# Rotary embedding by chunks with rows along the PSUM bank, its sine product moved to GpSimd, in a four-layer one-core Trainium2 kernel

## What is computed

```python
# layer 3; layer 1 adds a bias to q, k, v; layer 2 pairs even and odd elements of a head
q = x @ Wq   # 32 heads of 16;  k = x @ Wk, v = x @ Wv: 8 heads of 16
def rope(x):                      # before the scores, on q and k, not on v
    x1, x2 = x[..., :8], x[..., 8:]
    return concat([x1 * cos - x2 * sin, x2 * cos + x1 * sin])
out = softmax(causal(rope(q) @ rope(k).T / 4)) @ v @ Wo
```

## Time and profile before

| what | value |
|---|---|
| three runs, median | 2409.13 us (2407.0 to 2411.66) |
| profiled execution, its own time | 2416.49 us |
| its span | 2414.8 us |
| mean granted clock of PE | 0.963 |
| busy: PE, DVE, ACT, POOL | 2254.6, 1464.6, 1183.2, 506.3 us |

### The profile page before, as it was taken

How to read it: one execution, slowest core, us unless ns; L and a number is a source line. 1 busy time by engine, 2 the same in 40 slices (tenths; PEclk the granted TensorE clock), 3 DMA queues, 4 the chain that set the end, 5 groups by cost and what they waited for, 6 DMA issues and landing times.

```text
span 2414.8 us, 36047 instructions
## 1 busy us (share of the span) xinstructions
PE 2254.6 (93%) x12664; PEld 1220.6 (51%) x12664; DVE 1464.6 (61%) x3257; ACT 1183.2 (49%) x2273; POOL 506.3 (21%) x646
## 2 busy tenths in 40 slices
PE   6688898999999999999899999989898999999998
PEld 5455554545455455555555555545443444444443
DVE  6767787857667576787877778777752221221222
ACT  5465677645556465565666666576861101011010
POOL 4433323212312122131312222122220000000000
PEclk8699898999999999999999999999999999999999
DMA  5000324312313123231413133243323000000000
GB/s 179 1 1 19 104 82 164 103 47 72 117 42 114 35 58 120 80 108 53 144 53 112 54 106 116 78 122 98 100 61 97 0 18 0 14 5 5 13 1 18
DMA packets 135122, 163.59 MB, mean 68 GB/s; under 512 B 41616, under 2 KB 96912, under 8 KB 134672
## 3 DMA queue, kind: packets, MB, share of 16 engines
q1 hardware_dynamic: 134944, 161.29, 21.7%
HBM read 94.51 MB, written 53.35 MB: 61 GB/s over the span
## 4 chain that ended last, share of the span: by engine, by line
PE 76%; DMA 6%; DVE 6%; ACT 4%; SPq 3%; issue 2%; POOL 1%; ACTq 0%; POOLq 0%; DVEq 0%
PE ps L1505 15%; PE ps L1443 10%; PE ps L1516 7%; PE ps L1413 7%; PE ps L1397 7%; PE ps L1422 5%; PE ps L1458 5%; PE ps L1367 3%; PE ps L1286 3%; DMA scr_q<-big 3%; PE ps L1372 3%; PE ps L1467 2%; PE ps L1490 2%; PE ps L1378 1%; DVE peaks L2086 1%
## 5 line engine op out<-in xcount | busy, mean ns | idle before, releaser
L2086 DVE TENSOR_REDUCE peaks<-ps 128x4 f32<-128x512 f32 x960 | 625.0, 681 | 220.3 <-PE ps L1367 91.3
L1697 ACT ACTIVATE big<-ps 128x512 f32<-128x512 f32 x960 | 551.5, 603 | 362.7 <-PE ps L1397 252.9
L1901 POOL TENSOR_SCALAR_AFFINE_SELECT big<-big 128x512 f32<-128x512 f32 x384 | 248.3, 660 | 1010.6 <-ACT big L1697 1010.2
L1505 PE MATMUL ps<-xt,big 128*128 128x512 f32 x896 | 390.1, 593 | 2.8 <-issue 2.8
L1397 PE MATMUL ps<-big 99*128 99x512 bf16 (+3 forms) x1536 | 347.5, 305 | 23.5 <-ACT big L1697 18.2
L1443 PE MATMUL ps<-big,xt 128*128 128x512 f32 (+1 forms) x768 | 295.7, 497 | 0.5 <-DVE peaks L2086 0.2
L1505 PEld LDWEIGHTS ps<-xt,big 128*128 128x128 f32 x896 | 168.8, 190 | 209.3 <-issue 208.2
L1413 PE MATMUL ps<-big,vs 128*32 128x512 f32 (+3 forms) x3072 | 247.7, 450 | 11.5 <-POOL big L1901 8.2
L1786 ACT ACTIVATE t<-ps 128x512 f32<-128x512 f32 x56 | 33.5, 598 | 457.6 <-PE ps L1505 457.6
L1686 ACT ACTIVATE ps<-cbf 128x512 f32<-128x512 bf16 x384 | 230.8, 605 | 37.3 <-DVE peaks L2086 31.5
L2142 DVE SCALAR_TENSOR_TENSOR t<-rest,t 128x512 f32<-128x512 f32 x56 | 38.7, 691 | 280.4 <-PE ps L1505 276.8
(11 more groups left out here) (225 smaller groups left out, 2906.2 us busy)
## 6 DMA issues: line engine op xcount, KB each, us to landing
big<-scr_q SPq DMA_DIRECT2D x96, 384.0 KB, 4.1
scr_q<-big SPq DMA_DIRECT2D x48, 384.0 KB, 2.9
scr_q<-big SPq DMA_DIRECT2D x48, 256.0 KB, 3.1
recb<-scr_sums SPq DMA_DIRECT2D x96, 128.0 KB
big<-scr_k SPq DMA_DIRECT2D x48, 192.0 KB, 3.3
big<-in_ffn_gu SPq DMA_DIRECT2D x14, 512.0 KB, 6.2
scr_q<-big SPq DMA_DIRECT2D x48, 128.0 KB, 3.2
ctxt<-ots SPq DMA_DIRECT2D x192, 32.0 KB
```

The source lines that it names most:

```text
L1505: mm = pe.matmul(bank_of(kind, n, m), wgu[:, m // 2, c, way, m % 2 * P:(m % 2 + 1) * P], xt[:, c, :], start=(c == 0), stop=(c == DC - 1))
L1697: act.activation(probs[:, i * S:(i + 1) * S], bank_of("exp", g, i), ACT.Exp, scale=1.0 / 16 if attn_of(n) == 1 else 0.25).then_inc(made["p ...
L1901: pool.affine_select(block_, block_, [[0, GQ], [1, P]], ALU.is_ge, zero, base=0, channel_multiplier=-1).then_inc(made["cut"], 1)
L2086: dve.tensor_reduce(to, blocks, AX.X, ALU.max, negate=True).then_inc(made["negmax"], 1)
```

## The change

Queries and keys are now projected with the weights stationary and the tokens moving, so that a chunk comes out of PE with the tokens along the bank, one bank for each chunk. The transposes of `r` are gone. The values keep the old direction, as sixteen steps of 128 columns into one bank (`vproj`), between the second and the third chunk. For each chunk ACT copies the two halves of the bank crosswise into `r` (`swap`, two instructions on 64 partitions each), DVE multiplies the bank by the cosines into `t1` (`cosines`), POOL multiplies `r` by the sines in place (`sined`), DVE adds them (`rotate`), and the split into parts then reads `r` instead of a bank. The rotation tables now need the channels on partitions: PE turns the old table once for each of two tables (`tabs`) and ACT writes four pieces of 64 partitions to a new tile `cs` (`rotations`). The item `("tabs", 1)` and the load of the second table stand in `arrived`, behind the input rows; `("tabs", 2)` is added to the plan behind the last chunk of batch 3. "tabs" is put into FRONT. All chunks of batch n+1 now stand before the output product of batch n-1, not between its blocks.

```diff
-FRONT = ("inx", "inh", "th", "hm", "f", "hd")
+FRONT = ("tabs", "inx", "inh", "th", "hm", "f", "hd")
...
     if before >= 0:
-        first = first[:-len(CHUNKS)] if after < NIT else []
-        rest = [[(0.45, ("chunk", after, c))] for c in CHUNKS] if after < NIT else [[]] * len(CHUNKS)
         for j in range(TJ):
             first += [(0.86, ("dense", before, j, c)) for c in range(DC)]
-            first += [(0, ("y", "d", before, j))] + rest[j]
-        first += [(0, ("ln", "d", before))] + rest[TJ]
+            first += [(0, ("y", "d", before, j))]
+        first += [(0, ("ln", "d", before))]
...
         items += [("inx", b, c) for c in range(DC)] + [("inh", b)]
+    items += [("tabs", 1), ("load_rope", 2)]
     return items + [("tab", m) for m in range(1, 10)]
...
     items = [(0.45, ("xt", "a", n, c)) for c in range(DC)]
-    late = []
-    for j in range(TJ):
...
-    return items + [(0, i) for i in late] + [(0.45, ("chunk", n, c)) for c in CHUNKS]
+    for nth, c in enumerate(CHUNKS):
+        if nth == 2:
+            items += [(0.9, ("vproj", n, j)) for j in range(TJ)] + [(0, ("vals", n))]
+        items += [(0.86, ("proj", n, c, k)) for k in range(DC)] + [(0, ("chunk", n, c))]
+    return items
...
+    if kind == "tabs":
+        return [("PE", "tabs", k, TURN), ("ACT", "rotations", k, 2500)]
...
+        return [("ACT", "swap", k, 1250), ("DVE", "cosine", k, 730), ("POOL", "sined", k, 1280), ("DVE", "rope", k, 720),
+                ("ACT", "hi", k, ROWS_ACT), ("DVE", "rest", k, ROWS_DVE),
                 ("ACT", "mid", k, 660), ("POOL", "lo", k, 1250), ("SP", "cw", k, 2000)]
...
+    if name == "tabs":
+        return [("load_rope", k)]
+    if name == "rotations":
+        return [("tabs_full", k)] + ([("rope", (NB - 1, CHUNKS[-1]))] if n == 2 else [])
...
     if name == "load_rope":
-        return [("rope", (NB - 1, TJ - 1))]
+        return [("tabs_full", (1,))]
...
-        if kind == "rope" and item[1:] == (3, TJ - 1, 1):
-            plan.append(("load_rope", 2))
+        if kind == "chunk" and item[1:] == (3, CHUNKS[-1]):
+            plan.append(("tabs", 2))
...
+                mm = pe.matmul(bank_of("proj", n, c), wp[:, k, c * P:(c + 1) * P], xt[:, k, :], start=(k == 0), stop=(k == DC - 1))
...
+                for k in range(DC):
+                    mm = pe.matmul(bank_of("vproj", n)[:, j * P:(j + 1) * P], xt[:, k, j * P:(j + 1) * P], wp[:, k, QK:QKV],
+                                   start=(j == 0 and k == 0), stop=(k == DC - 1), skip_group_check=True)
...
+            def turn_tables(A):
+                pe.wait_ge(rope_in, 16 * A)
+                bank = bank_for("tabs", A)
+                turn_tiles(bank, lambda j: ropet[:, j].rearrange("p w k -> p (w k)")).then_inc(made["tabs_full"], 1)
...
+            def rotations(A):
+                act.wait_ge(made["tabs_full"], counted("tabs_full", A))
+                if A == 2:
+                    act.wait_ge(made["rope"], counted("rope", NB - 1, CHUNKS[-1]))
+                bank = bank_of("tabs", A)
+                act.activation(cs[0:64, 0, :], bank[0:64], ACT.Copy)
+                act.activation(cs[64:P, 0, :], bank[0:64], ACT.Copy)
+                act.activation(cs[0:64, 1, :], bank[64:P], ACT.Copy, scale=-1.0)
+                act.activation(cs[64:P, 1, :], bank[64:P], ACT.Copy).then_inc(made["rotations"], 1)
...
+                act.activation(r[0:64, c, :], bank[64:P], ACT.Copy)
+                act.activation(r[64:P, c, :], bank[0:64], ACT.Copy).then_inc(made["swap"], 1)
...
+                pool.tensor_tensor(r[:, c, :], r[:, c, :], cs[:, 1, :], ALU.mult).then_inc(made["sined"], 1)
...
+                if attn_of(n) == 1:
+                    dve.scalar_tensor_tensor(t1[:], bank, bias_c[:, c:c + 1], cs[:, 0, :], ALU.add, ALU.mult).then_inc(made["cosine"], 1)
+                else:
+                    dve.tensor_tensor(t1[:], bank, cs[:, 0, :], ALU.mult).then_inc(made["cosine"], 1)
...
+                dve.tensor_tensor(r[:, c, :], r[:, c, :], t1[:], ALU.add).then_inc(made["rope"], 1)
```

More of the change, by code:

```diff
@@ L213 @@
 TURN, ROWS_ACT, ROWS_DVE = 450, 640, 730
-HELD_BY = {"inx": "inx", "th": "ut", "f": "ft", "qx": "qx", "qm": "y16", "max": "negmax", "exp": "probs", "shift": "sh", "pv": "ot", "x3": "x3", "gate3": "z3", "up3": "h3", "xt": "xt", "chunk": "rest",
+HELD_BY = {"inx": "inx", "th": "ut", "f": "ft", "qx": "qx", "qm": "y16", "max": "negmax", "exp": "probs", "shift": "sh", "pv": "ot", "x3": "x3", "gate3": "z3", "up3": "h3", "xt": "xt", "proj": "cosine", "tabs": "rotations",
            "ag": "agc", "hw": "hw_out", "gate": "zt", "up": "ht"}
@@ L304, in pieces @@
         return [("PE", "xt", k, TURN), ("ACT", "xt", k, ROWS_ACT)]
[L305 to L308, removed]
+    if kind == "vals":
+        return [("DVE", "vadded", k, 750) if attn_of(k[0]) == 1 else ("ACT", "vfilled", k, 660)]
     if kind == "chunk":
-        return [("PE", "chunk", k, TURN), ("ACT", "hi", k, ROWS_ACT), ("DVE", "rest", k, ROWS_DVE),
+        return [("ACT", "swap", k, 1250), ("DVE", "cosine", k, 730), ("POOL", "sined", k, 1280), ("DVE", "rope", k, 720),
+                ("ACT", "hi", k, ROWS_ACT), ("DVE", "rest", k, ROWS_DVE),
                 ("ACT", "mid", k, 660), ("POOL", "lo", k, 1250), ("SP", "cw", k, 2000)]
@@ L331, with chunk_before, values @@
          "load_gu": 6500, "load_dn2": 4000}
+def chunk_before(n, c):
+    nth = CHUNKS.index(c)
+    return (n, CHUNKS[nth - 1]) if nth else (n - 1, CHUNKS[-1]) if n else None
+def values(n):
+    return "vadded" if attn_of(n) == 1 else "vfilled"
 def heads_free(n):
@@ L429, in order_of @@
         return ([("cut", (n, 2 * k[1]))]
-                + [("added" if attn_of(n // 8) == 1 else "filled", (n // 8, TJ - 1, 1))])
+                + [(values(n // 8), (n // 8,))])
     if name == "cut":
@@ L464, in order_of @@
     if name == "proj":
+        behind = [("vproj_full", (n,))] if k[1] == CHUNKS[-1] and k[2] == 0 else []
+        return [("xt", ("a", n, DC - 1)), ("load_proj", (attn_of(n),))] + behind
+    if name == "vproj":
         return [("xt", ("a", n, DC - 1)), ("load_proj", (attn_of(n),))]
[L466 to L473, removed]
-    if name == "rope":
[L475 to L479, removed]
-        return [("turned", k)] + late
-    if name == "chunk":
-        return [("rope", (n, TJ - 1))]
+    if name in ("vadded", "vfilled"):
+        return [("vproj_full", k), ("begin", ())] + ([("pv_full", (8 * n - 9, 1))] if n >= 2 else [])
+    if name == "tabs":
+        return [("load_rope", k)]
+    if name == "rotations":
+        return [("tabs_full", k)] + ([("rope", (NB - 1, CHUNKS[-1]))] if n == 2 else [])
+    if name == "swap":
+        late = [("y_full", ("f", n - 3, TJ - 1))] if k[1] == CHUNKS[1] and n >= 3 and attn_of(n - 3) < 3 else []
+        return [("proj_full", k)] + ([("rest", (n - 1, k[1]))] if n else []) + late
+    if name == "cosine":
+        before = chunk_before(n, k[1])
+        return [("proj_full", k), ("swap", k), ("rotations", (min(attn_of(n), 2),)), ("rope", before) if before else ("begin", ())]
+    if name == "rope":
+        return [("cosine", k), ("sined", k)]
+    if name == "sined":
+        return [("swap", k), ("rotations", (min(attn_of(n), 2),))]
     if name == "gate":
@@ L535, in order_of @@
         elif k[1] == 0:
[L536 removed]
+            late = [("proj_full", (NIT - 1, CHUNKS[-1]))]
         elif k[1] == 6:
@@ new lines, in add_values, with cosines @@
+                dve.tensor_tensor(vs[:, n % 2, :, :, 0:HD], bank_of("vproj", n).rearrange("p (j h d) -> p j h d", j=TJ, h=NKV),
+                                  bias_v[:].rearrange("p (h d) -> p h d", h=NKV).unsqueeze(1).broadcast_to((P, TJ, NKV, HD)),
+                                  ALU.add).then_inc(made["vadded"], 1)
+            def cosines(n, c):
+                dve.wait_ge(made["proj_full"], counted("proj_full", n, c))
+                dve.wait_ge(made["swap"], counted("swap", n, c))
+                dve.wait_ge(made["rotations"], counted("rotations", min(attn_of(n), 2)))
+                before = chunk_before(n, c)
+                if before:
+                    dve.wait_ge(made["rope"], counted("rope", *before))
@@ L2396, in flow_vectors @@
                         flow_norm(*k)
-                    elif kind == "added":
-                        fill(*k)
-                    elif kind == "turned":
-                        turn(*k)
+                    elif kind == "vadded":
+                        add_values(*k)
+                    elif kind == "cosine":
+                        cosines(*k)
                     elif kind == "rope":
-                        combine(*k)
+                        rotate(*k)
                     elif kind == "rest":
```

204 lines of the change are left out of this document (95 added, 109 removed).

## The result

The changed kernel takes 2430.76 us (median of 4 runs, 2427.11 to 2435.96) where the kernel before takes 2408.65 (4 runs): the ratio is 1.0092, 95% interval 1.0070 to 1.0114. It is slower, by 22 us between the medians and by 15.4 between the spans of the two profiled executions. The forecast was 2398 us, with most of the chance on faster.

A forecast was written before the change was run, and what follows sets the result against it. PE sets the pace from 480 to 1600 us, serial chains between engines before 480. The terms -24 + 4 - 22 - 8 + 35 + 4 sum to -11 us, 2409 to 2398 us, range 2362 to 2430.

The forecast's parts named there:

- transposes: Batches 1 to 11: five chunk transposes a batch go, 2.2 us of PE each batch, -24 us (bounds -22 and -31).
- gap at the end of the chunks: End of each batch's chunks: the slot wait closes, returning idle time and clock, -22 us (bounds 0 and -37).
- front, batch 0: Batch 0: keys are projected early, so writes and loads lie under the rest, -8 us (bounds 0 and -12).
- start: Kernel start: PE and ACT stand waiting for the rotation table to land, +35 us (bounds 30 and 38).
- bank: From 44 to about 600 us: the second table's transpose holds a PSUM bank, +4 us, +21 if idle time doubled.
- VectorE, ScalarE, GpSimd: In the batches: none is the bound, only a few meetings in position hurt, +4 us (bounds -4 and +15).
- POOL against DVE: In the batches: a POOL product holds up DVE's small SBUF work, not maxima or cosines, which read PSUM.
- projection: Each batch on PE: 25.2 us before, 24.8 to 25.3 after, so no difference.
- The gap stays: Rival 1, end of the chunks: first_part still waits for a slot, +11 us in sum, 2420 us, chance 0.22.
- The missing bank bites: Rival 3, front and first batches: one bank fewer loses 25 us, 2419 us, chance 0.09.
- GpSimd's product holds VectorE: Rival 4, in the batches: a third of 60 products meet DVE work, +27 us, 2425 us, chance 0.06.
- sums of `r` longer than 0.7 us: Sign named for the lock: DVE's sums of `r` in the chunks' rotation would take over 0.7 us.

The follow-up runs named there:

- gl_turned: Changed kernel with late table transposes and bias additions waiting for the shift's transpose, plus four transposes put back ahead of each query and key projection: 2360.96 us.
- gl_again: Changed kernel with late table transposes, the second held until batch 3 is rotated, and GpSimd's bias additions waiting for the shift's transpose: 2337.80 us, ratio to before 0.9730.
- late_both: Changed kernel with the first table's transpose behind the input transposes and the second's held back until batch 3 is rotated: 2378.09 us, ratio to before 0.9861.
- late_tabs: Changed kernel with table transposes moved behind the input transposes, the second still in the front and holding its bank: 2388.55 us, ratio to before 0.9914.
- before_gated: Kernel before the change, with only GpSimd's bias additions made to wait for the transpose of the shift behind the split: 2394.07 us, ratio 0.9936.
- gated: Changed kernel with GpSimd's bias additions made to wait for the transpose of the shift behind the split: 2393.22 us, ratio to before 0.9940.
- gl_sine: Changed kernel with late table transposes and waiting bias additions, plus the sines' product moved from GpSimd to VectorE: 2329.88 us, ratio to before 0.9682.

## Why the prediction was wrong, point by point

In the table, "measured" is worked out from the kernels above, by spans at exp and from dense 0 to 11 where these are given.

| term | forecast | measured | from |
|---|---|---|---|
| transposes | -24 | -22.4 | gl_turned less gl_again, dense 0 to 11 |
| gap at the end of the chunks, with the +4 of the other engines | -18 | -26.3 | 1335.2 - 1383.9 = -48.7, of which 22.4 are the row above |
| front, batch 0 | -8 | -10.6 | exp, late_both less before |
| start | +35 | +38.5 | exp, after less late_tabs |
| bank | +4 | +13 | exp, late_tabs less late_both |
| additions against the split | none | +24.9 | (1376.9 - 1335.2) - (1400.7 - 1383.9) |
| exp to dense 0, and the tail | none | -1.7 | rows of the first section |
| sum | -11 | +15.4 | |

The sum of the spans is exact by construction. Of its parts the transposes, the start, the bank and the additions each have an edit of their own. The gap's row has none: it is what is left of the batches when the others are taken off, and as the stretch holds the transposes of ten batches in the kernel before and those of nine in `gl_turned`, some 2 us of it belong to the row above. The front's row likewise holds all that changed for batch 0. The rows taken at exp carry the 7 us by which readings of the same instructions differ there.

The medians lie 22 us apart and not 15.4, since the profiled execution of the kernel before was 7.8 us above its median and that of the changed one 1.2. For the profiled execution the forecast was 2405.5; with the 26 us that the terms missed that is 2432, and 2431.95 was measured.

1. *What failed* is the step that took the other engines for +4 us in all ("VectorE, ScalarE, GpSimd", with "POOL against DVE"). It priced GpSimd's new product and put the additions that were already there, against VectorE's split, at nothing; they cost 24.9 us more than before. The gap beside it was forecast at -22, with the +4 at -18, and -26.3 is what is left for the two: the right cause and near in size, and the slot wait is gone. Together the batches were to become 42 us shorter (24 and 18), and became 23.8. I took what stood beside the gap in the list of waits (14.2 us for the split) as a constant, and read the earlier trace rows as a statement on the new product alone. The kernel before met the additions with the whole split in four batches and passed them in others, as at 928.61; the changed kernel met them in eight. The runs show what these meetings cost in both kernels; that it was the closed gap and the shorter batches that brought them about is argued from the two timelines alone. The question left out was which pairs of pieces pass each other narrowly, and what a shift by the length of the closed gap would do to them.
2. *The bank* was sized at +4 with +21 as its bound; it is +13, with the order that the planner makes of it. I looked for it from 250 to 480 us, where nearly all of it was over: it is complete at the first exponential (290.6 and 277.6), in the stretch of the state-space layers, which hold four of the banks.
3. *The start* was right in place, cause and nearly in size: first pieces at 39.43 and 42.98, first input transpose at 43.89. That this meets the forecast 43.9 so closely is luck: the first table landed 17.8 us after its issue and not 16.4, the second 2.4 us after its issue and not 4.0, and the two misses cancel. ScalarE's tanh came at 42.98 and not 41.3. At exp 38.5 us arrive, or 34.2 to 41.2 with the four readings of exp above, so the front's chains give nothing back that could be seen.
4. *Transposes, projection, front* were right: -22.4 for -24, 298.3 us for 301.9, and -10.6 for -8 (-5.3 to -14.5 with the other readings of exp, 282.9 in `before_gated` and 273.6 in `gl_again`). The first maxima come 27.8 us later (277.58), as named.
5. *The rivals.* "The gap stays" gave 2420 and had the right sign for a wrong reason. "The missing bank bites" is half true. "GpSimd's product holds VectorE" named the right lock and the wrong instruction: the product costs at most 8 us; the additions, which the change doesn't touch, cost 25 more than before. Its sign, sums of `r` longer than 0.7 us, came true (1.03 us on the mean in the changed kernel), but all but one of the long ones started beside GpSimd's other work and not beside the product.

## What to carry to other kernels

When an edit closes a stall, list the pairs of instructions on the other engines that pass each other within less than the stall's length, and ask which of them will meet once the rhythm is regular: here a lock that cost 15 us came to cost 36 to 39. A new piece of work needs its real arrival time in the planner, since a default of 0 for a load that lands at 39.3 us put both engines behind it for some 36 us. And before a run is read as evidence, compare the orders of instructions: an edit of a list that a planner sorts anew may be no edit at all.

## What the hardware showed that I had not expected

- VectorE steps of 32 columns, 0.18 to 0.19 us in `gated`, took 1.10 to 1.20 us one after the other while GpSimd ran four additions of 1.24 us: four short instructions were each held by one long one, 4.7 us for 0.7 us of work.
- A stall of TensorE cost about 1.6 times its length here: with 25.1 us of idle time gone from dense 0 to 11 the stretch was 40.2 us shorter, and the clock over the 10 us behind one such place was 1.00 instead of 0.66.
- Sums of two SBUF tiles (128x512) on VectorE took 0.68 us where they met nothing on GpSimd, and 1.37 us on the mean where they started beside GpSimd's third part of a chunk, itself 1.16 us long at the place shown; VectorE's products that read PSUM stayed at 687 and 688 ns in `gl_again` and `gl_sine`.
